# Key norms by a separate Newton run on GpSimd, scores per head in 64x64 tiles, and a new order of instructions in the windowed-attention stage

## What is computed

```python
def attn_layer(x, Wqkv, qs, ksc, Wo):          # x: (2, 2048, 128), 16 heads of 64
    q, k, v = split(x @ Wqkv)                  # each (2, 16, 2048, 64)
    q = l2norm(q) * qs
    k = l2norm(k) * ksc                        # t / max(norm(t), 1e-12), per row and head
    q = q * cos * scale + rotate_half(q) * sin * scale
    k = k * cos / scale + rotate_half(k) * sin / scale
    out = local_attention(q, k, v)             # windows of 32, each sees itself and the one before
    return out @ Wo
for i in range(6):
    x = attn_layer(shift_tokens(x), Wqkv[i], q_scale[i], k_scale[i], Wo[i]) + x
    x = ffn_layer(shift_tokens(x), ...) + x
```

## Time and profile before

| | before |
|---|---|
| median of 3 runs | 6257.24 us (6253.01 to 6261.46) |
| profiled execution | 6261.02 us, span 6259.3 us |
| TensorE matmul busy | 5185.6 us (83%) |
| VectorE busy | 4407.7 us (70%) |
| ScalarE busy | 3747.8 us (60%) |
| GpSimd busy | 2032.6 us (32%) |

### The profile page before, as it was taken

The page is one execution under the profiler, slowest core; times in us unless marked ns, Lnnn a source line. Parts: engine busy times, 40 slices in busy tenths (PEclk is TensorE's granted clock), DMA queues, the critical chain, the costliest instruction groups (busy, mean ns, idle before and its releaser), DMA issues. The chain is left out here.

```text
span 6259.3 us, 141962 instructions
## 1 busy us (share of the span) xinstructions
PE 5185.6 (83%) x41656; PEld 4217.9 (67%) x41656; DVE 4407.7 (70%) x11808; ACT 3747.8 (60%) x12063; POOL 2032.6 (32%) x1699
## 2 busy tenths in 40 slices
PE   5996959992499977999779997799968999699994
PEld 3665858982377766777667776677757777577773
DVE  4554666777477776777867777677777777677777
ACT  1112423341488855888568884688837888388882
POOL 0000000002244433444344442444424444244441
PEclk7876979996799999999999998999989999799997
DMA  0000200000011010000110001100010000100001
GB/s 18 0 0 14 59 9 1 0 0 31 23 23 23 22 41 23 22 22 22 42 24 22 22 22 42 24 22 22 22 44 22 22 22 22 44 22 22 22 22 48
DMA packets 103558, 144.77 MB, mean 23 GB/s; under 512 B 65414, under 2 KB 72859, under 8 KB 103131
## 3 DMA queue, kind: packets, MB, share of 16 engines
q1 hardware_dynamic: 94155, 109.63, 7.8%
q0 software_dynamic: 9232, 33.12, 1.6%
HBM read 49.13 MB, written 2.10 MB: 8 GB/s over the span
## 5 line engine op out<-in xcount | busy, mean ns | idle before, releaser
L1463 POOL TENSOR_TENSOR d_qk<-d_qk,d_sin_terms 128x512 f32<-128x512 f32 x792 | 995.1, 1277 | 1505.5 <-DVE d_sin_terms L1899 1505.5
L1782 ACT ACTIVATE d_probs<-d_S_ps,d_neg_max 128x96 f32<-128x96 f32 x3096 | 1016.2, 351 | 239.7 <-DVE d_neg_max L1928 239.7
L1899 DVE TENSOR_TENSOR d_qk<-d_A_ps,d_tables 128x512 f32<-128x512 f32 x816 | 564.4, 692 | 582.0 <-ACT d_squares L1745 581.9
L1469 POOL TENSOR_TENSOR d_qk<-d_qk,d_inv_norm 128x1024 f32<-128x1024 f32 x396 | 744.8, 1901 | 511.7 <-DVE d_inv_norm L1922 511.7
L1576 PEld LDWEIGHTS d_S_ps<-d_kT,d_q_blocks 128*128 128x128 f32 x6240 | 802.0, 192 | 4.1
L1576 PE MATMUL d_S_ps<-d_kT,d_q_blocks 128*128 128x96 f32 x6240 | 801.4, 271 | 0.0
L1782 ACT ACTIVATION_READ_ACCUMULATOR d_probs<-d_S_ps,d_neg_max 128x1 f32 x3096 | 671.7, 217 | 0.0
L1533 PE MATMUL d_A_ps<-d_wqkv_hi,d_xT_hi 128*128 128x512 f32 x1212 | 599.8, 495 | 18.1 <-DVE d_sin_terms L1899 13.4
L1540 PE MATMUL d_T_ps<-d_ident,d_qk 128*128 128x128 f32 x3168 | 504.2, 282 | 128.4 <-POOL d_qk L1469 105.7
L1899 DVE TENSOR_TENSOR d_sin_terms<-d_A_ps,d_tables 128x512 f32<-128x512 f32 x816 | 555.5, 681 | 0.0
L1586 PE MATMUL d_PT_ps<-d_ident,d_probs 128*96 128x128 f32 (+1 forms) x3072 | 473.9, 277 | 93.2 <-DVE d_probs L1937 93.2
(11 more groups left out here) (391 smaller groups left out, 10430.6 us busy)
## 6 DMA issues: line engine op xcount, KB each, us to landing
d_v_early<-d_v SPq DMA_DIRECT2D x198, 256.0 KB, 3.0
d_v_early<-d_v SPq DMA_DIRECT2D x198, 128.0 KB, 2.3
d_tables<-L_ffn_rotary POOLq DMA_DIRECT2D x7, 2048.0 KB, 9.7
d_qk<-L_ffn_Wqkv POOLq DMA_DIRECT2D x21, 512.0 KB, 4.2
d_xs<-d_xb SPq DMA_DIRECT2D x96, 63.5 KB
d_xs<-d_xb SPq DMA_DIRECT2D x48, 127.0 KB
ax_fp_blocks<-L_ffn_blocks_gu SPq DMA_DIRECT2D x16, 256.0 KB, 3.9
ax_fp_scales<-L_ffn_scales_gu SPq DMA_DIRECT2D x64, 64.0 KB, 3.5
```

The costliest lines, as they stand in the source:

```text
L1463: nc.gpsimd.tensor_tensor(c4[:, :, s, :], c4[:, :, s, :], s4[:, :, 1 - s, :], ALU.add).then_inc(rotated, 1)
L1469: nc.gpsimd.tensor_tensor(r3, r3, rn[:, b, k, :].unsqueeze(2).broadcast_to([P, HEADS, HD]), ALU.mult).then_inc(scaled, 1)
L1782: nc.scalar.activation(pr[:, g, n, seen_columns(g)], S[g % 2][:, n * SEEN:(n + 1) * SEEN], ACT.Exp, bias=nmax[:, g, n:n + 1], accum_out=de ...
L1899: nc.vector.tensor_tensor(terms[:, k, cols].rearrange("p (h d) -> p h d", d=HD), A[(c + 1) % 2][:].rearrange("p (h d) -> p h d", d=HD), ta ...
```

## The change

Three things change, all in the attention half.

The sums of squares of keys and queries are treated apart. GpSimd floors the key sums itself (`floor_k`), ScalarE makes the start value in a new instruction (`guess_k`), and GpSimd runs ten dependent steps on 16 columns (`newton_k`: a third-order step, then a second-order one). VectorE's nine Newton steps stay, on 16 query columns instead of 32. `front` is split: GpSimd rotates and scales the keys first, then copies the x tile, rotates and scales the queries, and ends its body with floor and Newton for the keys of the tile after.

`scores` issues two matmuls per unit, one per head: weight 64 x 64 (the head's 64 rows of a plain copy `qT`), 96 columns, output in the head's 64 partitions. The block-diagonal buffer goes, and `drain_q_T` is one 128 x 512 copy instead of two of 64 x 512.

The bodies of TensorE, ScalarE and VectorE are written in another order.

```diff
+                def floor_k(l, u):
+                    pool.wait_ge(ssq_ready, l * SUMS_IN_LAYER + (u * 2 + 1))
+                    pool.sem_inc(waits_met)
+                    nc.gpsimd.tensor_scalar(k_sums[:], ssq[:, 1, :, 0], 1.0e-24, None, ALU.max).then_inc(k_floor, 1)
+                def newton_k(n, b):
+                    pool.wait_ge(k_guess, n + 1)
+                    nc.gpsimd.tensor_tensor(k_work[:, 0, :], k_sums[:], k_root[:], ALU.mult).then_inc(k_newton, 1)
+                    pool.wait_ge(k_newton, n * K_STEPS + 1)
+                    nc.gpsimd.tensor_tensor(k_work[:, 1, :], k_work[:, 0, :], k_root[:], ALU.mult).then_inc(k_newton, 1)
...
+                    pool.wait_ge(k_newton, n * K_STEPS + 9)
+                    nc.gpsimd.tensor_tensor(k_inv[:, b, :], k_work[:, 2, :], k_work[:, 3, :], ALU.mult).then_inc(k_newton, 1)
...
-                    front(f0, l, 0, 0)
+                    floor_k(l, 0)
+                    newton_k(l * XS, 0)
+                    rotate(l, 0, 1)
+                    rotate(l, 0, 0)
+                    scale_k(f0, l * XS, 0)
+                    scale_q(f0, 0)
+                    floor_k(l, 1)
+                    newton_k(l * XS + 1, 1)
                     split_w1(l)
...
+                                f1 = f0 + (u + 1)
+                                rotate(l, u + 1, 1)
+                                scale_k(f1, l * XS + (u + 1), 1 - b)
                                 pool.wait_ge(xT_ps, l * XS + (u + 2))
                                 nc.gpsimd.tensor_copy(xcur[:], xs[:, bass.ds(j + 1, 1), b, :].rearrange("p j d -> p (j d)")
                                                       ).then_inc(x_tile_ready, 1)
-                                front(f0 + (u + 1), l, u + 1, 1 - b)
+                                rotate(l, u + 1, 0)
+                                scale_q(f1, 1 - b)
+                                floor_k(l, u + 2)
+                                newton_k(l * XS + (u + 2), b)
...
                     for n in range(UNITS):
                         p, half = unit(g, n)
-                        last = nc.tensor.matmul(S[g % 2][:, n * SEEN:(n + 1) * SEEN], qx[:, p, half, :],
-                                                kT[b][jj][:, p, HALF * half:HALF * half + SEEN], start=False,
-                                                stop=True, skip_group_check=True)
+                        for head in range(2):
+                            rows = slice(HD * head, HD * head + HD)
+                            last = nc.tensor.matmul(S[g % 2][rows, n * SEEN:(n + 1) * SEEN], qT[rows, p, HALF * half:HALF * half + HALF],
+                                                    kT[b][jj][rows, p, HALF * half:HALF * half + SEEN], start=False,
+                                                    stop=True, skip_group_check=True)
...
                                 project(l, u + 1, 4)
+                                project(l, u + 1, 5)
                                 scores(l, u, 2, b, jj, (j + (J - 1)) // J)
-                                project(l, u + 1, 5)
                                 transpose_x(l, u + 2)
+                                transpose_k(f1, 0)
                                 transpose_probs(a, 0)
                                 scores(l, u, 3, b, jj, 0)
+                                transpose_k(f1, 1)
                                 attend(l, a, j, 0, b, jj)
+                                project(l, u + 2, 0)
                                 transpose_probs(a, 1)
-                                transpose_k(f1, 0)
+                                project(l, u + 2, 1)
+                                transpose_q(f1, 0)
                                 attend(l, a, j, 1, b, jj)
-                                project(l, u + 2, 0)
                                 transpose_probs(a, 2)
-                                transpose_k(f1, 1)
-                                project(l, u + 2, 1)
-                                transpose_probs(a, 3)
-                                transpose_q(f1, 0)
-                                attend(l, a, j, 2, b, jj)
+                                scores(l, u + 1, 0, b1, jj1, (j + (b + (J - 1))) // J)
                                 project(l, u + 2, 2)
                                 transpose_q(f1, 1)
-                                scores(l, u + 1, 0, b1, jj1, (j + (b + (J - 1))) // J)
+                                attend(l, a, j, 2, b, jj)
+                                transpose_probs(a, 3)
+                                scores(l, u + 1, 1, b1, jj1, 0)
                                 attend(l, a, j, 3, b, jj)
                                 project(l, u + 2, 3)
-                                scores(l, u + 1, 1, b1, jj1, 0)
                                 project_out(a)
...
+                def guess_k(n):
+                    act.wait_ge(floor_set, 2)
+                    act.wait_ge(k_floor, n + 1)
+                    act.wait_ge(k_newton, n * K_STEPS)
+                    rsqrt_guess(nc, k_sums[:], k_root[:], guess_offset[:, 0:1]).then_inc(k_guess, 1)
...
-                    nc.scalar.activation(qx[0:HALF, 4 * half:4 * half + 4, :, 0:HALF],
-                                         T0[0:HALF, :].rearrange("p (c s t) -> p c s t", c=4, s=2), ACT.Copy
-                                         ).then_inc(q_T_low, 1)
-                    nc.scalar.activation(qx[HALF:P, 4 * half:4 * half + 4, :, HALF:P],
-                                         T0[HALF:P, :].rearrange("p (c s t) -> p c s t", c=4, s=2), ACT.Copy
-                                         ).then_inc(q_T_high, 1)
+                    nc.scalar.activation(qT[:, 4 * half:4 * half + 4, :], T0[:].rearrange("p (c t) -> p c t", c=4), ACT.Copy
+                                         ).then_inc(q_T_ready, 1)
...
                                 exps(l, u, 1)
-                                guess(f1)
                                 drain_v(l, u + 1, 4, b1, jj1)
                                 drain_v(l, u + 1, 5, b1, jj1)
+                                guess(f1)
+                                split_x(l * XS + (u + 2))
+                                drain_k_T(f1, 0, b1, jj1)
                                 drain_probs(a, 0)
-                                split_x(l * XS + (u + 2))
                                 exps(l, u, 2)
+                                drain_k_T(f1, 1, b1, jj1)
                                 drain_attention(a, 0)
+                                square(l, u + 2, 0)
                                 drain_probs(a, 1)
...
                                 normalise(l, u, 0)
+                                find_max(l, u, 2)
                                 newton_steps(f1, 1 - b)
-                                find_max(l, u, 2)
+                                split_x_low(l * XS + (u + 2))
                                 normalise(l, u, 1)
                                 find_max(l, u, 3)
-                                split_x_low(l * XS + (u + 2))
                                 normalise(l, u, 2)
+                                turn(l, u + 2, 0, j + 1)
+                                sum_squares(l, u + 2, 1)
```

More of the change, by code:

```diff
@@ L1129 @@
 MASKED = -1.0e30
+CUBIC = 8.0 / 3.0
+K_STEPS = 10
 HALF = 64
@@ L1223, in windowed_transformer @@
         den = m.sb("den", [P, 4, UNITS])
-        rt2 = m.sb("newton_step", [P, 2 * HEADS])
-        sums_ps, root_ps, step_ps = (Y[:, D + 2 * HEADS * i:D + 2 * HEADS * (i + 1)] for i in range(3))
-        rden = Y[:, D + 6 * HEADS:D + 7 * HEADS].rearrange("p (g n) -> p g n", g=4)
+        rt2 = m.sb("newton_step", [P, HEADS])
+        sums_ps, root_ps, step_ps = (Y[:, D + HEADS * i:D + HEADS * (i + 1)] for i in range(3))
+        rden = Y[:, D + 3 * HEADS:D + 4 * HEADS].rearrange("p (g n) -> p g n", g=4)
         pT = m.sb("probsT", [P, 2, UNITS * P])
@@ L1463, in rotate @@
                         nc.gpsimd.tensor_tensor(c4[:, :, s, :], c4[:, :, s, :], s4[:, :, 1 - s, :], ALU.add).then_inc(rotated, 1)
-                def scale(f, k, b, scaled):
-                    pool.wait_ge(newton, f * RSQRT_STEPS + RSQRT_STEPS)
+                def floor_k(l, u):
+                    pool.wait_ge(ssq_ready, l * SUMS_IN_LAYER + (u * 2 + 1))
+                    pool.sem_inc(waits_met)
+                    nc.gpsimd.tensor_scalar(k_sums[:], ssq[:, 1, :, 0], 1.0e-24, None, ALU.max).then_inc(k_floor, 1)
@@ L1467, in scale, with scale_k @@
+                def scale(f, k, inverse, scaled):
                     pool.wait_ge(rotated, f * 4 + (4 - 2 * k))
                     r3 = raw[:, k, :].rearrange("p (h d) -> p h d", d=HD)
-                    nc.gpsimd.tensor_tensor(r3, r3, rn[:, b, k, :].unsqueeze(2).broadcast_to([P, HEADS, HD]), ALU.mult
+                    nc.gpsimd.tensor_tensor(r3, r3, inverse.unsqueeze(2).broadcast_to([P, HEADS, HD]), ALU.mult
                                             ).then_inc(scaled, 1)
-                def front(f, l, u, b):
```

(27 more changed lines are left out.)

76 lines of the change are left out of this document (43 added, 33 removed).

## The result

The changed kernel takes **5998.77 us** (median of 4 runs, 5998.52 to 6003.16) against 6255.12 us before (4 runs, 6250.91 to 6261.46): ratio 0.9591, 95% interval 0.9574 to 0.9608, 256 us less. 5978 was forecast, with a range of 5885 to 6205. Its profiled execution has a span of 5996.9 us.

What follows compares the result with a forecast made beforehand. No engine full: a body is TensorE's work plus late hand-overs. Body 19.47 to 17.8 us saves 321 over 192 bodies, layer heads add 42: 6261 - 321 + 42 = 5982, 3.8 lower for the median: 5978 us; range 5885 to 6205.

Steps and rivals of the forecast that it cites:

- The four waits go, none takes their place: TensorE's waits before `transpose_x`, second `transpose_probs` and both `transpose_k`, together 2.12 us a body, all go.
- TensorE's work, 17.32 + 0.25 = 17.57: TensorE's work in a body without waits, 17.32 us, plus about 0.25 for the new score tiles.
- the cost of the tile form: TensorE changing tile form around a score group: 0.22 us in all, read from `attend` and the transposes before it.
- The query copies, "nothing by itself, but what lets ScalarE keep up": One query copy for two saves ScalarE 1.4 us a body; no gain itself, but lets it follow a shorter body.
- 0.2 for late hand-overs: Allowance of 0.2 us a body for ScalarE's drains before scores and the last `attend`, each behind an `exps`.
- The list-by-list layout: The four engines' new lists laid side by side with prices: all four waits go, closest hand-overs 0.2 to 0.4 spare.
- The loop's turn, 0.03 a body: 0.03 us added to every body for the turn of the loop.
- GpSimd's steps, 0.25 apiece: Ten dependent 16-column Newton steps for keys on GpSimd: 0.25 us each with hand-over, 2.5 us in all.
- The rival with a chance of 0.06: GpSimd's chain sets the body, 13.65 + 10p; binds from 0.42 us a step, a loss from 0.56; chance 0.06.
- The head of a layer, 7 us each: At each layer's start GpSimd's Newton runs delay keys and the next x tile: 7 us a layer, 42 in all.
- The rival on the other side, tiles one after another: The two heads' score tiles do not overlap: 1.33 us a group for 0.70, body 20.3, 6458 us; chance 0.10.

Runs made afterwards that it cites:

- split alone: Kernel before with only the keys' Newton run moved to GpSimd and 16 columns left on VectorE; 6270.97 us, ratio 1.0018.
- order without the split: Changed kernel with keys and queries sharing one 32-column Newton run on VectorE; new order, small score tiles and single query copy kept; 7255.5 us, ratio 1.1592.
- the tiles alone: Kernel before with only the 64x64 score tiles and the single plain query copy; 6282.66 us, ratio 1.0036.
- the kernel without the tiles: Changed kernel with block-diagonal scores and two query copies as before; split Newton run and new order kept; 6076.61 us, ratio 0.9706.

## Why the prediction was right, step by step

It was right about the mechanism of the plain body. Its number came out by luck, through errors that cancel.

- **The four waits go, none takes their place** (2.12 us): right, for the order and the split together. By plain bodies: before 19.35, split alone 19.26, order without the split 24.13 (with the tiles), both 17.91, both with the tiles 17.20. Neither half is worth much by itself; one makes the other possible.
- **TensorE's work, 17.32 + 0.25 = 17.57**: it is 17.20. The score groups were priced against 4 x 0.98 = 3.92, but in the timeline of before mask and scores take 4.26 of a body, since two of the groups stand 0.96 before the next row, part of which I had booked to `attend`. Now they take 4.27: the term is 0.01, not 0.25. The group itself was priced well (1.09, measured 1.08), as were a pair (0.088, measured 0.083, where the 128 x 128 weight of before took 0.108 for the same 96 columns) and the cost of the tile form (0.22, measured 0.10 at the mask and about 0.15 at the scores). The six projections take 4.66 for 4.82, since two of them now follow each other (0.77 and 0.70): 0.16 that I hadn't seen.
- **The query copies, "nothing by itself, but what lets ScalarE keep up"**: right, and now with a size: 0.70 us a plain body, or 78 us in all together with what the turns differ by.
- **0.2 for late hand-overs**: none in a plain body, where TensorE has no idle time. The list-by-list layout held.
- **The loop's turn, 0.03 a body**: the step that failed. It is (19.92 - 17.20) / 4 = 0.68 in the changed kernel, 0.13 in the one before. The forecast's body was 0.6 too long without a turn and left out 0.6 a body for the turns: hence 17.8. What the runs showed in its place is TensorE standing 2.0 us at each turn for nothing that the profile shows and, behind 12 of 42 of them, then running at a granted clock of 0.50; the loop written out takes 2.37 of the 2.71 away.
- **GpSimd's steps, 0.25 apiece**: 0.348. I priced the operation (0.21, measured 0.22) well and the hand-over too low: 0.08 to 0.20 instead of 0.04. The ten cost 3.5 us, not 2.5. It costs nothing in the body by a margin of 0.07 to 0.16 us. The rival with a chance of 0.06 was much nearer than that: by this margin one more step, 0.30, would have brought it in, an estimate; two did. Start to start, GpSimd took 0.348 / 0.21 = 1.66 times as long as VectorE for the same width.
- **The head of a layer, 7 us each**: 9.0. Before the first keys, the timeline at the second layer shows scaling begin at 2358.20 and TensorE idle for it (the last fence is the same place before):

```profile
2348.89 0.60 ACT L1794 ACTIVATE d_squares<-d_A_ps 128x512 f32<-128x512 f32 x1 [0.68 <-PE d_A_ps L1586]
...
2353.36 4.88 POOL L1469 TENSOR_TENSOR d_qk<-d_qk,d_sin_terms 128x512 f32<-128x512 f32 x4
2358.20 1.90 POOL L1506 TENSOR_TENSOR d_qk<-d_qk,d_k_inv_norm 128x1024 f32<-128x1024 f32 x1
```
```profile
2360.24 1.11 PE L1591 MATMUL d_T_ps<-d_ident,d_qk 128*128 128x128 f32 x4 [7.76 <-POOL d_qk L1506]
```
```profile
2411.62 1.09 PE L1540 MATMUL d_T_ps<-d_ident,d_qk 128*128 128x128 f32 x4 [5.09 <-POOL d_qk L1469]
```

  The last square before them starts at 2348.89, so the first keys are turned 11.35 after it. Before, with the square of the earlier trace rows at 2402.95 and the transposes at 2411.62, it was 8.67: 2.7 later, where 1.9 was forecast. Two chains of ten steps, each 1.0 us longer than priced, would make up the missing 2.0, an estimate, and with two steps more in each the heads grew by 1.1. That the chains are all of it isn't shown: the heads are 6.2 longer with the split alone, and 4.3 longer with the new order and no Newton run on GpSimd at all.
- **The rival on the other side, tiles one after another**: refuted. The two heads' records start 7 ns apart, a pair every 83 ns, into one bank, in other partitions. With the two heads' matmuls apart the second head starts 0.39 late and the kernel is 0.3% slower than before, but even then the tiles overlap.
- **The range**: its ends come to 5880 and 6209 and were both rounded inward. Nothing hangs on it.

## What the runs showed that I had not expected

- **The longer loop body was paid for at the turn.** With sixteen score records a group for eight, TensorE's queue of instructions carried 8 packets of 16 KB a turn more, in the old order and in the new, and TensorE stood 1.9 to 2.1 us at the turn; behind 12 of the 42 in the changed kernel, and 14 of 42 with the tiles alone, it then ran at a granted clock of 0.50. With eight (`x41656` records) there were none. ScalarE stood as long (2.0 us) in the kernel without the tiles, with 12267 records, and not in the changed kernel with 11871. All six kernels with `q8 instruction: 459` have turns that cost 1.2 to 2.7 us; of the others only the one with ScalarE's wait (1.41) has a turn over 0.52. Writing the loop out removed the stall, though packets still came (363). Why the packets come in every turn of the longer loop and not of the shorter one, and what TensorE stands for there, was not shown.
- **More packets need not lengthen the turn.** The split alone has `q14 instruction: 308` as well, and its turn costs 0.42, no more than before. ScalarE's longest idle time there is 1.3 us on average, 0.6 in the body behind the turn, but the profile ends it with VectorE's `find_max` at all but 2 of 42 turns. That a stall hides in it is my reading and not shown.
- **A gap cost more than its length.** With one Newton run for both, 4.47 us of idle time made the body 6.9 us longer; the other 2.46 are rows run at the lower clock (granted 0.50) behind it.
- **The two small tiles overlapped best when they came in turn.** Same work, same bank, other order: 1.18 against 0.81 a group, since the second tile started 0.39 later.

## What to carry to other kernels

Read the single distances of a line that runs once per body, not only their mean: a mean that fits the forecast can hold a body that is too fast and a turn that is too slow. When an edit adds instructions to a loop's list, look at the instruction queues on the page and at "issue" at the turn, and try the loop written out. An order and the dependence that it relies on have to be tested together; here the split alone took 0.5% off a plain body, the order without it (and with the tiles) made it 25% longer, and both together, without the tiles, took 7% off it.
